# Cross attention on one core: a tile's first mixes held back, the finished tile's end spread over the next tile

## The chip, the cores and the metric

The kernel runs on one core of a Trainium2 chip: TensorE (matrix products), VectorE, ScalarE and GpSimd as compute engines, SyncE issuing the transfers. The metric is the device time of one launch in microseconds (us). Shown are the median of three runs and, for everything that is read in detail, one profiled execution.

## The reference, cut to what matters

A decoder of two layers on 4 x 256 tokens of width 256. The change touches one of its six blocks, the cross attention of layer 1. It treats all tokens as one sequence: 1024 queries against 1024 context rows, 16 heads of 16 columns.

```python
q = _fq_sym(q, axis=-1)          # rounded to 127 levels a head and token
k = _fq_sym(k, axis=-1)
v = _fq_sym(v, axis=2)
attn = jnp.einsum('bhqd,bhkd->bhqk', q, k)
attn = jax.nn.softmax(attn.astype(jnp.float32), axis=-1)
attn = _fq_unsigned(attn, axis=-1)   # rounded to 255 levels
out = jnp.einsum('bhqk,bhkd->bhqd', attn, v)
out = jnp.transpose(out, (0, 2, 1, 3)).reshape(B, N, C)
return out @ Wp + bp
```

The result is added to the residual stream x, whose normalised form feeds the routed experts.

## The kernel before, in words

`decoder` runs its blocks one behind the other. `cross_attention` (L1115) has two parts: `quantise` (L1133) makes the rounded queries, keys and values, and `attend` (L1309) does the rest. All of the change is in `attend`.

The 1024 queries are 8 tiles (NT) of 128. A unit u is one head of one tile: u = 16 t + h, 128 units in all. A unit passes through five stations:

- score (L1362, TensorE): two products of 512 columns, from the queries and keys of the head, into one of SCORED = 3 buffers of the accumulator memory. It waits until the exponential of unit u - 3 is done.
- row maximum and bias (L1424, VectorE): `c_neg_max` (L1427), then `c_bias` (L1429).
- exponential (L1416, ScalarE): scaled to 255 levels and written as 16-bit integers (`c_probs`), which rounds it; the sum of the row is read out behind it.
- cast (L1357, GpSimd) to bf16, then a transposing transfer (L1349, issued by SyncE) into `c_pT`, a ring of TURNED = 10 heads.
- mix (L1372, TensorE): eight small products (L1378) of the transposed head with the values, into 16 columns of `mixed`. The 16 heads of a tile fill 256 columns of one buffer, and there is only one such buffer.

When the 16 mixes of a tile are done, the tile is finished in five steps:

- `normalise` (L1432, VectorE): reciprocal of the row sums (L1434), and a multiply (L1438) that reads `mixed` and writes `c_o`. The first mix of the next tile waits for it (L1376), since it overwrites `mixed`.
- `finish_a` (L1382, TensorE): two turnings (L1387) into the buffer `tail`.
- `scale_values` (L1443, VectorE): two operations (L1448) from `tail` to `c_oT`.
- `finish_b` (L1390, TensorE): the projection in 32-bit floats (L1393) and its bias (L1394), into `tail` again.
- `residual` (L1451, VectorE): adds `tail` to x (L1453), then the statistics for the next normalisation (L94, L96).

Each engine works through its own list, which is written out by hand; the engines meet at semaphores alone. TensorE's list (L1396 to L1407) has for each u: score(u), then mix(u - 8) (MIX_LAG = 8), then, behind the mix of head 3 of a tile, `finish_a` of the tile before, and behind that of head 7 `finish_b`. VectorE's list (L1457 to L1469) has row_max(u), then behind unit 16 t + 8 `normalise`, behind 16 t + 11 `scale_values`, behind 16 t + 14 `residual`, each for tile t - 1. ScalarE, GpSimd and SyncE have nothing but the 128 units.

Of the kernel before, what the change touches and what calls it, by code (L numbers as in the profile page):

```python
# [18 lines left out]
NT = N // P  # L19
# [70 lines left out]
def norm_statistics(nc, eng, sh, t):  # L90


    ln = sh.ln
    nc.vector.bn_stats(ln.stats[:, t, :], sh.x[:, t, :]).then_inc(ln.steps, 1)  # L94
    if t >= 1:
        nc.vector.bn_aggr(ln.mv[:, t - 1, :], ln.stats[:, t - 1, :]).then_inc(ln.steps, 1)  # L96
        ln.step_count += 1
    ln.step_count += 1
    eng.wait_ge(ln.steps, ln.step_count)
    if t == NT - 1:  # L100
        nc.vector.bn_aggr(ln.mv[:, t, :], ln.stats[:, t, :]).then_inc(ln.steps, 1)
        ln.step_count += 1
        eng.wait_ge(ln.steps, ln.step_count)
        nc.vector.tensor_scalar(ln.rstd[:, :], ln.mv[:, :, 1], LN_EPS, None, ALU.add).then_inc(ln.var_ready, 1)  # L104
# [986 lines left out]
HEADS_C = 16  # L1091
# [23 lines left out]
def cross_attention(nc, sh, i):  # L1115
    with ExitStack() as ctx:
        sb, ps, sem = scope(nc, ctx, "c0_")
        s = Buffers()

        s.qT = sb("qT", [P, WC, N], BF16)  # L1120
        s.kT = sb("kT", [P, WC, N], BF16)
        s.v = sb("v", [P, NT, D], BF16)
        s.q_scale = sb("q_scale", [P, NT, HEADS_C])
        s.v_scale = sb("v_scale", [P, DC])
        s.identb = sb("identb", [P, P], BF16)
        s.w_p = sb("w_p", [P, DC, D])
        s.b_p = sb("b_p", [1, D])
        s.ones = sb("ones", [1, P])
        quantise(nc, sh, s, i)
        attend(nc, sh, s)  # L1130
# [178 lines left out]
def attend(nc, sh, s):  # L1309
# [4 lines left out]
    with ExitStack() as ctx:  # L1314
# [1 line left out]
        SCORED = 3  # L1316
        RING = 4
        ROUNDED = 6
        TURNED = 10
        MIX_LAG = 8  # L1320
        LOG_LEVELS = float(np.log(LEVELS_P))
        UNITS_C = NT * HEADS_C
        probs = sb("probs", [P, RING, N], I16)
        rounded = sb("rounded", [P, ROUNDED, N], BF16)
        pT = sb("pT", [P, TURNED, NT, P], BF16)
        neg_max, bias = sb("neg_max", [P, NT, HEADS_C]), sb("bias", [P, NT, HEADS_C])
# [5 lines left out]
        scored, bias_ready, exp_done, rounded_ready = sem("scored"), sem("bias_ready"), sem("exp_done"), sem("rounded_ready")  # L1332
        turned = [sem("turned%d" % n) for n in range(TURNED)]
        mixed_ready, o_ready, oT_ready, oT_copied, out_ready, out_added = (
            sem("mixed_ready"), sem("o_ready"), sem("oT_ready"), sem("oT_copied"), sem("out_ready"), sem("out_added"))

        def turned_count(u):

            return 16 * (u // TURNED + 1)

        block = ctx.enter_context(nc.Block())

        @block.sync
        def _(sp):
            for u in range(UNITS_C):
                sp.wait_ge(rounded_ready, u + 1)
                if u >= TURNED:
                    sp.wait_ge(mixed_ready, u - TURNED + 1)
                sp.dma_start_transpose(pT[:, u % TURNED, :, :], rounded[:, u % ROUNDED, :]).then_inc(turned[u % TURNED], 16)  # L1349

# [9 lines left out]
        @block.tensor  # L1360
        def _(pe):
            def score(u):  # L1362
                t, h = divmod(u, HEADS_C)
                if u >= SCORED:
                    pe.wait_ge(exp_done, u - SCORED + 1)
                at = slice(h % 2 * P // 2, (h % 2 + 1) * P // 2)
                for n in range(2):
                    last = nc.tensor.matmul(scores[:, u % SCORED, n, :], s.qT[at, h // 2, t * P:(t + 1) * P],  # L1368
                                            s.kT[at, h // 2, n * HALF:(n + 1) * HALF], start=True, stop=True)
                last.then_inc(scored, 1)  # L1370

            def mix(u):  # L1372
                t, h = divmod(u, HEADS_C)
                pe.wait_ge(turned[u % TURNED], turned_count(u))
                if h == 0 and t >= 1:
                    pe.wait_ge(o_ready, t)  # L1376
                for n in range(NT):
                    last = nc.tensor.matmul(mixed[:, 0, h * HD_C:(h + 1) * HD_C], pT[:, u % TURNED, n, :],  # L1378
                                            s.v[:, n, h * HD_C:(h + 1) * HD_C], start=(n == 0), stop=(n == NT - 1))
                last.then_inc(mixed_ready, 1)  # L1380

            def finish_a(t):  # L1382
                pe.wait_ge(o_ready, t + 1)
                if t >= 1:
                    pe.wait_ge(out_added, t)
                for c in range(DC):
                    last = nc.tensor.transpose(tail[:, 0, c * P:(c + 1) * P], o[:, c * P:(c + 1) * P], ident[:, :])  # L1387
                last.then_inc(oT_ready, 1)

            def finish_b(t):  # L1390
                pe.wait_ge(oT_copied, t + 1)
                for c in range(DC):
                    nc.tensor.matmul(tail[:, 0, 0:D], oT[:, c, :], s.w_p[:, c, :], start=(c == 0), stop=False)  # L1393
                nc.tensor.matmul(tail[:, 0, 0:D], s.ones[:, :], s.b_p[:, :], start=False, stop=True).then_inc(out_ready, 1)  # L1394

            for u in range(UNITS_C + MIX_LAG):  # L1396
                if u < UNITS_C:
                    score(u)
                if u >= MIX_LAG:
                    mix(u - MIX_LAG)  # L1400
                    t, h = divmod(u - MIX_LAG, HEADS_C)
                    if h == 3 and t >= 1:
                        finish_a(t - 1)
                    if h == 7 and t >= 1:
                        finish_b(t - 1)
            finish_a(NT - 1)
            finish_b(NT - 1)  # L1407
# [12 lines left out]
        @block.vector  # L1420
        def _(dve):
            chain = sh.chain.on(dve)

            def row_max(u):  # L1424
                t, h = divmod(u, HEADS_C)
                dve.wait_ge(scored, u + 1)
                chain.step(nc.vector.tensor_reduce(neg_max[:, t, h:h + 1], scores[:, u % SCORED, :, :].rearrange("p a b -> p (a b)"),  # L1427
                                                   AX.X, ALU.max, negate=True))
                nc.vector.tensor_scalar(bias[:, t, h:h + 1], neg_max[:, t, h:h + 1], s.q_scale[:, t, h:h + 1], LOG_LEVELS,  # L1429
                                        ALU.mult, ALU.add).then_inc(bias_ready, 1)  # L1430

            def normalise(t):  # L1432
                dve.wait_ge(exp_done, HEADS_C * (t + 1))
                chain.step(nc.vector.reciprocal(row_sum[:, t, :], row_sum[:, t, :]))  # L1434
                dve.wait_ge(mixed_ready, HEADS_C * (t + 1))
                if t >= 1:
                    dve.wait_ge(oT_ready, t)
                nc.vector.tensor_tensor(o[:, :].rearrange("p (h d) -> p h d", d=HD_C),  # L1438
                                        mixed[:, 0, 0:D].rearrange("p (h d) -> p h d", d=HD_C),
                                        row_sum[:, t, :].rearrange("p (h o) -> p h o", o=1).broadcast_to([P, HEADS_C, HD_C]),  # L1440
                                        ALU.mult).then_inc(o_ready, 1)

            def scale_values(t):  # L1443
                dve.wait_ge(oT_ready, t + 1)
                if t >= 1:
                    dve.wait_ge(out_ready, t)
                for c in range(DC):
                    last = nc.vector.tensor_scalar(oT[:, c, :], tail[:, 0, c * P:(c + 1) * P], s.v_scale[:, c:c + 1], None, ALU.mult)  # L1448
                last.then_inc(oT_copied, 1)

            def residual(t):  # L1451
                dve.wait_ge(out_ready, t + 1)
                nc.vector.tensor_tensor(x[:, t, :], x[:, t, :], tail[:, 0, 0:D], ALU.add).then_inc(out_added, 1)  # L1453
                dve.wait_ge(out_added, t + 1)
                norm_statistics(nc, dve, sh, t)

            for u in range(UNITS_C):  # L1457
                row_max(u)
                t, h = divmod(u, HEADS_C)
                if t >= 1:  # L1460
                    if h == MIX_LAG:
                        normalise(t - 1)
                    if h == MIX_LAG + 3:
                        scale_values(t - 1)
                    if h == MIX_LAG + 6:
                        residual(t - 1)
            normalise(NT - 1)
            scale_values(NT - 1)
            residual(NT - 1)  # L1469
# [459 lines left out]
```

## Time and profile before

| | |
|---|---|
| median of 3 runs | 1270.38 us (1269.29 to 1270.54) |
| the profiled execution | 1268.92 us |
| its span | 1267.1 us |
| `attend` in it | 862 to 1098 us, 236 us |
| the routed experts behind it | 1098 to 1267 us, 169 us |
| busy between 862 and 1098 us | TensorE 194.5 us, VectorE 189.1, ScalarE 165.8, GpSimd 133.2 |

The page gives busy time over the whole span, in which TensorE has 77% and VectorE 67%. For this change the stretch of `attend` counts: its table of stretches says how busy each engine was, at which TensorE clock (PEclk, 1.00 being full speed) and with which share of the transfer engines. In the timeline a row is one instruction or a few merged ones: start, duration, engine, line, operation and tiles, and in brackets how long the engine had stood idle and what released it. TensorE's rows appear twice, as PE (the product) and PEld (the load of its stationary operand). Matmul ends are modelled, so starts are what to go by.

### The profile page before, as it was taken

The page shows a single profiled execution, that of the slowest core. Times are in us where ns is not written, and L with a number is a line of the kernel's source. Part 1 is how long each engine was busy: PE and PEld are TensorE (multiplying, and loading weights), DVE is VectorE, ACT ScalarE, POOL GpSimd, SP SyncE. Part 2 cuts the span into 40 slices and gives each one's busy share as a digit, 9 for nine tenths or more (in the row PEclk, how much of TensorE's full clock was granted, in tenths as well). Part 3 has the DMA queues.
Part 4 walks back from the last instruction along what each step waited for, and adds up shares of the span by engine and source line. Part 5 has one row for each costly group of instructions (what it writes and reads, how often), then busy time and mean ns, then how long its engine had stood idle before and what let it go on. Part 6 is the DMA issues. An engine that isn't in the chain of part 4 may idle for free. (4 is left out here: it accounts for less than half of the span.)

```text
span 1267.1 us, 14674 instructions
## 1 busy us (share of the span) xinstructions
PE 978.5 (77%) x5537; PEld 647.1 (51%) x5537; DVE 852.1 (67%) x1192; ACT 598.8 (47%) x693; POOL 466.5 (37%) x278
## 2 busy tenths in 40 slices
PE   5669897349878889798989666877888888676990
PEld 2334743138777778687873255442222232355770
DVE  4663303999999999999702566687888788342442
ACT  2113032675866876777600233258777767311220
POOL 1133003855555555555000022205555555231004
PEclk9769989569898899898998979795555555568995
DMA  3020020000000000000002000946877876214113
GB/s 116 1 67 1 5 100 1 0 1 1 1 1 1 1 1 1 1 1 1 1 1 88 1 1 1 333 107 121 154 150 150 142 159 135 58 46 156 64 51 116
DMA packets 155448, 73.95 MB, mean 58 GB/s; under 512 B 138813, under 2 KB 151297, under 8 KB 154178
## 3 DMA queue, kind: packets, MB, share of 16 engines
q1 hardware_dynamic: 153842, 68.81, 21.5%
q0 software_dynamic: 1536, 4.20, 1.1%
q8 instruction: 45, 0.74, 0.2%
q14 instruction: 25, 0.20, 0.1%
HBM read 27.90 MB, written 11.53 MB: 31 GB/s over the span
## 5 line engine op out<-in xcount | busy, mean ns | idle before, releaser
L677 PE MATMUL r_head_sum<-ident,r_w 128*128 128x128 f32 (+1 forms) x2048 | 243.3, 283 | 41.7 <-DVE x L781 22.5
L677 PEld LDWEIGHTS r_head_sum<-ident,r_w 128*128 128x128 f32 (+1 forms) x2048 | 241.7, 199 | 48.4 <-issue 48.2
L631 POOL TENSOR_TENSOR r_pair_sum<-r_sims 128x2025 f32<-128x2025 f32 x39 | 142.1, 3646 | 148.8 <-DVE r_w L766 93.4
L1357 POOL CAST c_rounded<-c_probs 128x1024 bf16<-128x1024 int16 x128 | 133.2, 1040 | 156.2 <-ACT c_probs L1416 156.2
L1416 ACT ACTIVATE c_probs<-c_scores,c_bias,c_q_scale 128x1024 int16<-128x1024 f32 x128 | 154.2, 1205 | 61.3 <-DVE c_bias L1429 52.4
L1427 DVE TENSOR_REDUCE c_neg_max<-c_scores 128x1 f32<-128x1024 f32 x128 | 155.5, 1215 | 17.0 <-PE c_scores L1368 16.7
L775 DVE SCALAR_TENSOR_TENSOR r_w<-r_w,r_scale,r_z 128x2025 f32<-128x2025 f32 x64 | 148.0, 2314 | 7.9 <-PE r_z L645 7.0
L1368 PE MATMUL c_scores<-c_kT,c_qT 64*128 64x512 bf16 x256 | 129.9, 612 | 17.8 <-ACT c_probs L1416 14.3
L766 DVE SCALAR_TENSOR_TENSOR r_w<-r_pair_sum,r_kept,r_w 128x2025 f32<-128x2025 f32 x39 | 130.6, 3350 | 2.3 <-ACT r_w L703 2.2
L711 ACT ACTIVATE r_w<-r_w 128x2025 f32<-128x2025 f32 x64 | 116.1, 1882 | 4.2 <-DVE r_w L775 4.1
L1378 PEld LDWEIGHTS c_mixed<-c_v,c_pT 128*128 128x128 bf16 x1024 | 37.1, 106 | 124.8 <-issue 118.7
L703 ACT ACTIVATE r_w<-r_pair_sum,r_neg_max 128x2025 f32<-128x2025 f32 x39 | 76.8, 1981 | 34.4 <-PE r_head_sum L677 24.0
L653 PE MATMUL r_head_sum<-r_up,r_wT 128*128 128x256 f32 (+1 forms) x256 | 62.5, 406 | 16.1 <-ACT r_wT L731 16.1
L118 POOL TENSOR_TENSOR ln_rstd<-ln_rstd,ln_minus_half 128x8 f32<-128x8 f32 x6 | 9.9, 1646 | 163.8 <-DVE ln_rstd L104 155.5
L1378 PE MATMUL c_mixed<-c_v,c_pT 128*128 128x16 bf16 x1024 | 48.0, 177 | 23.4 <-DVE c_o L1438 17.4
L653 PEld LDWEIGHTS r_head_sum<-r_up,r_wT 128*128 128x128 f32 (+1 forms) x256 | 51.5, 204 | 25.5 <-ACT r_wT L731 17.8
L645 PE MATMUL r_z<-r_down,r_hT 128*128 128x512 f32 (+1 forms) x64 | 36.9, 729 | 32.5 <-DVE r_w L775 32.5
L631 POOL TENSOR_TENSOR xT<-r_sims 128x2025 f32<-128x2025 f32 x13 | 49.2, 3781 | 30.4 <-DVE r_w L766 30.4
L1791 DVE TENSOR_TENSOR e_gated<-e_hidden,e_gated 128x176 f32<-128x176 f32 x40 | 13.7, 342 | 65.7 <-ACT e_gated L1785 65.7
L631 POOL TENSOR_TENSOR ctxT<-r_sims 128x2025 f32<-128x2025 f32 x12 | 45.5, 3792 | 27.6 <-DVE r_w L766 27.6
L1686 POOL DMA_INDIRECT e_row<-expert_rows,e_place x16 | 15.3, 958 | 100.3 <-DMA expert_rows<-e_made 95.7
L1736 PE MATMUL e_hidden<-ew_w,e_rowT 128*128 x128 | 43.2, 460 | 0.0
(275 smaller groups left out, 1559.8 us busy)
## 6 DMA issues: line engine op xcount, KB each, us to landing
ew_w<-in_w SPq DMA_DIRECT2D x2, 2992.0 KB, 14.2
sorted_rows<-ew_w SPq DMA_DIRECT2D x1, 4096.0 KB, 40.2
e_row<-sorted_rows SPq DMA_DIRECT2D x8, 512.0 KB, 8.3
expert_rows<-e_made SPq DMA_DIRECT2D x8, 512.0 KB, 2.9
ew_w<-in_w_near SPq DMA_DIRECT2D x1, 2176.0 KB, 24.1
ctxT<-in_ctxT SPq DMA_DIRECT2D x2, 1024.0 KB, 8.8
r_up<-in_up SPq DMA_DIRECT2D x1, 2048.0 KB, 10.1
c_pT<-c_rounded SPq DMA_TRANSPOSE x128, 2.8
```

Source lines behind the costliest of these rows:

```text
L631: nc.gpsimd.tensor_tensor(sums[u % SUMS].rearrange("p (a b) -> p a b", b=KEYS), a.broadcast_to([P, KEYS, KEYS]), b.broadcast_to([P, KEYS, ...
L653: last = nc.tensor.matmul(head_sum[:, 0, 0:D], wT[0:k, b, :], r.up[0:k, b, :], start=(b == 0), stop=(b == PB - 1))
L677: last = nc.tensor.matmul(head_sum[0:m, b // 4, (b % 4) * P:(b % 4 + 1) * P], w[:, u % RING, b * P:b * P + m], ident[:, :], start=(h == 0 ...
L703: nc.scalar.activation(w[:, u % RING, :], sums[u % SUMS], ACT.Exp, bias=neg_max[:, t % 2, h:h + 1]).then_inc(exp_done, 1)
L711: nc.scalar.activation(w[:, u % RING, :], w[:, u % RING, :], ACT.Silu).then_inc(silu_done, 1)
L766: nc.vector.scalar_tensor_tensor(w[:, u % RING, :], sums[u % SUMS], kept[:, t % 2, h, TOP - 1:TOP], w[:, u % RING, :], ALU.is_ge, ALU.mult ...
L775: nc.vector.scalar_tensor_tensor(w[:, u % RING, :], w[:, u % RING, :], scale[:, t % 2, h:h + 1], z[:, :, :].rearrange("p a b -> p (a b)")[ ...
L1357: nc.gpsimd.tensor_copy(rounded[:, u % ROUNDED, :], probs[:, u % RING, :]).then_inc(rounded_ready, 1)
L1368: last = nc.tensor.matmul(scores[:, u % SCORED, n, :], s.qT[at, h // 2, t * P:(t + 1) * P], s.kT[at, h // 2, n * HALF:(n + 1) * HALF], sta ...
L1378: last = nc.tensor.matmul(mixed[:, 0, h * HD_C:(h + 1) * HD_C], pT[:, u % TURNED, n, :], s.v[:, n, h * HD_C:(h + 1) * HD_C], start=(n == 0 ...
L1416: nc.scalar.activation(probs[:, u % RING, :], scores[:, u % SCORED, :, :].rearrange("p a b -> p (a b)"), ACT.Exp, bias=bias[:, t, h:h + 1] ...
L1427: chain.step(nc.vector.tensor_reduce(neg_max[:, t, h:h + 1], scores[:, u % SCORED, :, :].rearrange("p a b -> p (a b)"), AX.X, ALU.max, neg ...
```

## The change

The first two mixes of a tile (HELD = 2) are left out at their place and done in pairs at heads 2 and 3: behind score 16 t + 10 come mixes 0 and 1, behind 16 t + 11 mixes 2 and 3, and from head 4 on it is one mix a unit again. `finish_a` goes from behind the mix of head 3 to behind that of head 4, `finish_b` from head 7 to head 9. On VectorE `normalise` stays behind row maximum 16 t + 8; `scale_values` goes from behind 16 t + 11 to 16 t + 14, and `residual` from 16 t + 14 to 16 t + 19, which is in the next tile; the one that falls off the end of the loop is done behind it. The ring of transposed heads grows from 10 to 13.

```diff
--- before.py
+++ after.py
@@ -1316,8 +1316,10 @@
         SCORED = 3
         RING = 4
         ROUNDED = 6
-        TURNED = 10
+        TURNED = 13
         MIX_LAG = 8
+        HELD = 2
+        TURN_AT, SCALE_AT, PROJECT_AT, ADD_AT = 4, 6, 9, 11
         LOG_LEVELS = float(np.log(LEVELS_P))
         UNITS_C = NT * HEADS_C
         probs = sb("probs", [P, RING, N], I16)
@@ -1334,6 +1336,14 @@
         mixed_ready, o_ready, oT_ready, oT_copied, out_ready, out_added = (
             sem("mixed_ready"), sem("o_ready"), sem("oT_ready"), sem("oT_copied"), sem("out_ready"), sem("out_added"))
 
+        def mixes_at(h):
+
+            if h < HELD:
+                return ()
+            if h < 2 * HELD:
+                return 2 * (h - HELD), 2 * (h - HELD) + 1
+            return (h,)
+
         def turned_count(u):
 
             return 16 * (u // TURNED + 1)
@@ -1397,11 +1407,12 @@
                 if u < UNITS_C:
                     score(u)
                 if u >= MIX_LAG:
-                    mix(u - MIX_LAG)
                     t, h = divmod(u - MIX_LAG, HEADS_C)
-                    if h == 3 and t >= 1:
+                    for m in mixes_at(h):
+                        mix(t * HEADS_C + m)
+                    if h == TURN_AT and t >= 1:
                         finish_a(t - 1)
-                    if h == 7 and t >= 1:
+                    if h == PROJECT_AT and t >= 1:
                         finish_b(t - 1)
             finish_a(NT - 1)
             finish_b(NT - 1)
@@ -1456,14 +1467,15 @@
 
             for u in range(UNITS_C):
                 row_max(u)
-                t, h = divmod(u, HEADS_C)
-                if t >= 1:
-                    if h == MIX_LAG:
+                if u >= MIX_LAG + HEADS_C:
+                    t, h = divmod(u - MIX_LAG, HEADS_C)
+                    if h == 0:
                         normalise(t - 1)
-                    if h == MIX_LAG + 3:
+                    if h == SCALE_AT:
                         scale_values(t - 1)
-                    if h == MIX_LAG + 6:
+                    if h == ADD_AT:
                         residual(t - 1)
+            residual(NT - 2)
             normalise(NT - 1)
             scale_values(NT - 1)
             residual(NT - 1)
```

## Rows read from the trace of the kernel before

**Rows 1.** Table of stretches: us; busy us (instructions) of each engine; PEclk; DMA share; GB/s.

```profile
880.00:890.00 10.00, 9.76 (x72) 2.99 (x72) 9.75 (x15) 9.41 (x15) 7.62 (x8) 0.50 0.95 170
944.00:972.00 28.00, 23.66 (x163) 8.24 (x161) 22.80 (x39) 19.76 (x32) 15.88 (x16) 0.50 0.73 150
```

**Rows 2.** Timeline, a unit at even pace: start us, us, engine, line, operation.

```profile
915.20 1.21 ACT L1416 ACTIVATE c_probs<-c_scores,c_bias,c_q_scale 128x1024 int16<-128x1024 f32 x1
...
916.46 1.21 DVE L1427 TENSOR_REDUCE c_neg_max<-c_scores 128x1 f32<-128x1024 f32 x1
...
916.55 1.03 PE L1368 MATMUL c_scores<-c_kT,c_qT 64*128 64x512 bf16 x2
...
917.71 0.21 DVE L1429 TENSOR_SCALAR c_bias<-c_neg_max,c_q_scale 128x1 f32<-128x1 f32 x1
917.84 1.21 DVE L1427 TENSOR_REDUCE c_neg_max<-c_scores 128x1 f32<-128x1024 f32 x1
```

**Rows 3.** Timeline, the normalising of a tile, and the next one's multiply.

```profile
924.74 0.24 DVE L1434 RECIPROCAL c_row_sum<-c_row_sum 128x16 f32<-128x16 f32 x1
...
925.02 0.42 DVE L1438 TENSOR_TENSOR c_o<-c_mixed,c_row_sum 128x256 f32<-128x256 f32 x1
...
925.59 0.36 PE L1378 MATMUL c_mixed<-c_v,c_pT 128*128 128x16 bf16 x8 [2.48 <-DVE c_o L1438]
...
926.95 1.22 DVE L1427 TENSOR_REDUCE c_neg_max<-c_scores 128x1 f32<-128x1024 f32 x1 [1.50 <-PE c_scores L1368]
...
928.46 1.21 ACT L1416 ACTIVATE c_probs<-c_scores,c_bias,c_q_scale 128x1024 int16<-128x1024 f32 x1 [2.30 <-DVE c_bias L1429]
...
953.98 0.42 DVE L1438 TENSOR_TENSOR c_o<-c_mixed,c_row_sum 128x256 f32<-128x256 f32 x1
```

**Rows 4.** Timeline, TensorE at its own pace, then turning and scaling.

```profile
927.16 1.03 PE L1368 MATMUL c_scores<-c_kT,c_qT 64*128 64x512 bf16 x2
...
928.44 1.03 PE L1368 MATMUL c_scores<-c_kT,c_qT 64*128 64x512 bf16 x2
...
930.24 1.03 PE L1368 MATMUL c_scores<-c_kT,c_qT 64*128 64x512 bf16 x2
...
931.09 0.60 DVE L1448 TENSOR_SCALAR c_oT<-c_tail,c_v_scale 128x128 f32<-128x128 f32 x2
```

**Rows 5.** Timeline, projection and residual of the first tile, and those of the seventh.

```profile
906.53 0.38 PE L1378 MATMUL c_mixed<-c_v,c_pT 128*128 128x16 bf16 x8
...
909.91 1.03 PE L1368 MATMUL c_scores<-c_kT,c_qT 64*128 64x512 bf16 x2
...
910.87 0.38 PE L1378 MATMUL c_mixed<-c_v,c_pT 128*128 128x16 bf16 x8
...
1080.70 1.20 ACT L1416 ACTIVATE c_probs<-c_scores,c_bias,c_q_scale 128x1024 int16<-128x1024 f32 x1
...
1083.73 0.42 DVE L1453 TENSOR_TENSOR x<-x,c_tail 128x256 f32<-128x256 f32 x1 [3.06 <-PE c_tail L1394]
...
1084.73 1.22 DVE L1427 TENSOR_REDUCE c_neg_max<-c_scores 128x1 f32<-128x1024 f32 x1
...
1086.23 1.21 ACT L1416 ACTIVATE c_probs<-c_scores,c_bias,c_q_scale 128x1024 int16<-128x1024 f32 x1 [4.24 <-DVE c_bias L1429]
```

**Rows 6.** List of waits, 860 to 1096 us: total us, times, longest us.

```profile
ACT c_probs L1416 <- DVE c_bias L1429: 52.4, 22, 4.2
DVE x L1453 <- PE c_tail L1394: 21.5, 7, 3.1
```

**Rows 7.** Table of stretches, the scores between a normalising and a turning.

```profile
928.00:934.00 6.00, 6.00 (x51) 2.14 (x50) 5.86 (x11) 4.78 (x7) 3.12 (x3) 0.50 0.69 152
```

**Rows 8.** Transposing transfers (ns min/median/max; landing), and the last mix in the timeline.

```profile
L1349 SPq DMA_TRANSPOSE c_pT<-c_rounded x128: 1231/1232/2688, 865.2 to 1088.7; - x128
...
DMA to landing us min/median/max: 2.7/2.8/5.3
...
1091.43 0.38 PE L1378 MATMUL c_mixed<-c_v,c_pT 128*128 128x16 bf16 x8 [5.13 <-DMA c_pT<-c_rounded]
```

## The prediction

> **What bounds the kernel now.** The table of stretches comes first. The attention stage runs from about 862 to 1098 us (the table of times), and the diff touches nothing outside it. While a tile's end is in the stretch (944 to 972 us), no engine is full: TensorE is busy 23.66 of 28 us, VectorE 22.80, ScalarE 19.76, the transfers 0.73 of the time. Between 880 and 890 us, where no finished tile is in the way, VectorE is busy 9.75 of 10 us [rows 1]. So the stage has an even pace and something that interrupts it.
>
> The timeline gives the pace [rows 2]. Row maxima start at 916.46 and 917.84, 1.38 us a head. VectorE sets it: row maximum, bias 1.25 us behind it (917.71), the next row maximum 0.13 us behind that, which is 0.08 us less than the bias's own 0.21 us. An exponential starts 1.50 us after its row maximum (926.95 to 928.46) [rows 3]. A score starts 1.35 us after the exponential three heads earlier (915.20 to 916.55), takes 1.03 us, and lies 1.29 us ahead of its row maximum (916.55 to 917.84). TensorE needs less than the pace when nothing holds it: 1.28 us from score to score (927.16 to 928.44) [rows 4], of which 0.96 goes by before the mix (909.91 to 910.87) [rows 5] and 0.32 is the mix.
>
> The timeline around a tile's end gives the interruptions, which have the same lengths in all seven tiles. First, normalising [rows 3]: VectorE is free at 924.74, and the next row maximum starts at 926.95, 2.21 us late; TensorE stood 2.48 us before the mix at 925.59, because the mix may not overwrite the sums that VectorE still reads, and the score is queued behind that mix. Second, scaling occupies VectorE from 931.09 for 0.60 us [rows 4], less the 0.08 us of hand-over: 0.52 us. Third, VectorE stands 3.06 us before the residual, waiting for the projection, which holds TensorE from the mix at 906.53 to the next score at 909.91; exponentials at 1080.70 and 1086.23 are 5.53 us apart, so 4.15 us are lost [rows 5]. Sum 6.88 us a tile; with 16 x 1.38 = 22.08 this is 28.96, and two normalisations are 925.02 and 953.98 apart, 28.96 [rows 3]. The list of waits agrees: ScalarE waited 52.4 us for the bias and VectorE 21.5 us for the projection [rows 6].
>
> **The change, part by part.** No instruction is added or removed; the arithmetic and the transfers are the same 128 heads. Only orders, and a ring of 13 instead of 10, change. I go through one tile with the figures above. Heads are counted on from the finished tile's successor: head 8 is the ninth of the new tile; head 16 on belong to the tile after.
>
> *Normalising, with the first two mixes held back.* VectorE's work keeps its place behind row maximum 8: 0.28 us from the reciprocal to the multiply (924.74 to 925.02) [rows 3], and then the multiply's 0.42 us less about 0.08 us of hand-over, 0.35 us; together 0.63 us, with 0.80 as the upper bound (full durations and a hand-over). The wait for it stood before score 9. It now stands behind score 10. Put score 8 at 0: row maximum 8 at 1.29, normalised tile ready at 1.29 + 1.38 + 0.28 + 0.42 = 3.37. Scores 9 and 10 start at 1.38 and 2.76, so the first mix asks at 2.76 + 0.96 = 3.72. It doesn't wait, but by only 0.3 us. Cost left: 0.63 instead of 2.21. The two held mixes are paid back as pairs, 0.96 + 2 x 0.32 = 1.60 us for heads 10 and 11; TensorE was ahead by 0.63 us because VectorE stood, so this hides. It costs if that lead is gone: 2 x 0.22 us.
>
> *Turning,* from behind mix 3 to behind mix 4. It put score 930.24 at 1.80 us behind score 928.44 instead of 1.28, so it costs 0.52 us of TensorE [rows 4]. Right after the pairs there is less lead than before: scores 10 to 13 start at 2.76, 4.36, 6.15, 7.95, and row maximum 13 can't start before 8.99, where VectorE was free at 8.82: 0.17 us lost.
>
> *Scaling,* behind row maximum 14: 0.52 us of VectorE, as before.
>
> *Projection,* from behind mix 7 to behind mix 9, that is behind score 17. Its length on TensorE is 909.91 - 906.53 - 0.32 = 3.06 us [rows 5]. Its stall is no longer behind VectorE's wait for the residual. Score 17 at 0: row maxima 17 and 18 are due at 1.29 and 2.67, but score 18 starts only at 0.96 + 0.32 + 3.06 = 4.34 and ends at 5.38: 2.71 us. From it goes the delay of 0.52 us that scaling has just put on VectorE, and which TensorE, 3 heads ahead at most, takes as lead: 2.19 us.
>
> *Residual,* now behind row maximum 19. It has its input, so VectorE spends its own work on it: 1083.73 to the next row maximum at 1084.73, 1.00 us [rows 5]. Before, this was hidden in the projection's stall; now it is paid, since after the stall TensorE makes a head per 1.28 us and VectorE is the late one again.
>
> *Sum for a tile:* 0.63 + 0.17 + 0.52 + 2.19 + 1.00 = 4.51, against 6.88; 22.08 + 4.51 = 26.6 us against 28.96. Both engines' own sums are under it: TensorE 16 x 1.28 + 0.52 + 3.06 = 24.1, VectorE 22.08 + 0.63 + 0.52 + 1.00 = 24.2. For the tile finished during the last one, projection and residual fall behind the last score; TensorE stands there anyway, 5.13 us before the last mix, for its transposed head [rows 8]. It pays 0.63 + 0.17 + 0.52 = 1.32. Saved: 6 x 2.37 + (6.88 - 1.32) = 14.2 + 5.6 = 19.8 us. The last tile's own end, from the exponential at 1086.23 on, is unchanged.
>
> *The ring of 13* lets held heads lie longer. A transpose waits for the mix 13 heads back instead of 10, and a mix is held back by two heads at most, so this wait is looser than now. Landing takes 2.8 us, 5.3 at most [rows 8]. A mix comes 1.35 + 5 x 1.38 + 0.96 = 9.2 us after its exponential starts; exponential, cast (less than a head's 1.38, since GpSimd keeps the pace) and landing take 1.35 + 1.38 + 2.8 = 5.5. Cost nothing, and nothing at 5.3 us either.
>
> *Bounds.* A paired mix can cost 0.32 to 0.40 us (0.38 is a mix's recorded length [rows 5]), which makes +3.3 us over the stage; the projection may overlap more or less, 2.7 to 3.4 us for 3.06, for -2 to +2; normalising at 0.80 makes +1.3. Together about -3 to +6 us on the sum.
>
> The profiled execution took 1268.92 us, 1.46 below the median of the runs. 1268.92 - 19.8 = 1249.1, and 1250.5 against the median.
>
> **Rivals.**
> *Clock.* All of this goes at TensorE's lower level, 1.2 GHz: granted clock 0.50 [rows 1]. If denser work raised it to 2.4 GHz, the projection would take about half (1.5 us) and its stall nearly vanish. The tile would cost 22.08 + 0.63 + 0.52 + 1.00 + about 0.2 = 24.4: saved 6 x 4.5 + 5.7 = 33 us, 1237. Against it: from 928 to 934 us TensorE was busy for 6.00 of 6.00 us, in this same mixture, and the clock stayed at 0.50 [rows 7].
> The Trainium skill, "TensorE: Matmul & The Clock Gate", Part 1 (The HAM clock gate), says that sustained TensorE activity lifts the throttle to 2.4 GHz; by that rule the result would be this rival's. The trace disagrees in that stretch, and I go with it.
>
> *The stall only moves.* If row maxima 18 and 19 come as late as row maximum 15 does now, for instance because the mixes and the projection leave TensorE no lead at all, the projection costs 4.15 and the residual 1.00 on top: 0.63 + 0.17 + 0.52 + 5.15 = 6.47 a tile, saved 6 x 0.42 + 5.6 = 8 us: 1262. Against: what made it 4.15 is that row maximum 15 waits behind a residual that waits for the projection, and this order is gone.
>
> *Transposes become the bound: slower.* They go through one queue, each waiting for its forerunner, and today's pauses let the queue drain: one landing took 5.3 us [rows 8]. With fewer pauses a backlog could reach the mixes. A landing must exceed 9.2 - 2.7 = 6.5 us to delay a mix, and the queue must need more than 26.6 / 16 = 1.66 us a head to set the pace, 28.96 / 16 = 1.81 to be slower than now; at 1.9 us the stage would take 7 x 1.4 = 10 us longer: 1280. Against: an issue takes 1.23 us (median; one took 2.69), the transfers' share between 880 and 890 us, at full pace, is 0.95, and the longest landing of the whole stage stayed under that.
>
> **How the numbers follow.** Forecast 0.82, clock 0.05, stall only moves 0.09, transposes 0.04. The forecast is the likeliest: 1250.5. Its bounds give 1247 to 1256; the range is 1245 to 1257, and the rivals lie outside with 0.18. A measurement of this kernel can tell about 0.2% (2.5 us) from no change. Faster: forecast, clock and the moved stall together 0.95; same 0.02 (a moved stall with the bounds against it), slower 0.03.
>
> **What would show it.** Normalisations 26.6 us apart. TensorE idle before a tile's first mix gone (2.48 us there, to nothing), VectorE's wait before the residual gone (21.5 us to almost nothing), and in its place row maxima that wait about 2.2 us for a score right after the projection. ScalarE's gaps about 0.6, 0.2, 0.5, 2.2 and 1.0 us a tile. The stage after keeps its 169 us. I am wrong if the mix waits for the normalised tile after all (its margin is 0.3 us), if the granted clock leaves 0.50, or if mixes wait for transposes.

## The result and the profile after

The changed kernel takes 1249.36 us (median of 4 runs, 1248.58 to 1250.83), against 1270.46 us before; the ratio is 0.9836, 95% interval 0.9819 to 0.9853. The forecast was 1250.5 us. The profiled execution took 1249.71 us, 19.2 us less than the profiled one of before, with a span of 1247.8 us.

| | before | after |
|---|---|---|
| `attend` in the trace | 862 to 1098 us, 236 us | 862 to 1078 us, 216 us |
| the routed experts behind it | 169 us | 170 us |
| two normalisations apart | 28.96 us | 26.64 us |
| ScalarE waited for the bias | 52.4 us | 33.9 us |
| VectorE waited at the residual, tiles 1 to 7 | 21.5 us | 1.9 us |
| TensorE waited for the normalised tile | 2.48 us a tile | 0 |

The whole difference lies in `attend`: from its first exponential to its last it takes 19.5 us less (223.4 us before, 203.9 after). The table of stretches of the kernel after, cut at its borders (the columns as in [rows 1]):

```profile
0.00:862.00 862.00, 666.68 (x3670) 492.86 (x3670) 600.28 (x688) 402.41 (x354) 299.37 (x111) 0.88 0.09 31
862.00:1078.00 216.00, 193.09 (x1338) 66.46 (x1338) 188.56 (x311) 165.74 (x256) 133.15 (x128) 0.50 0.79 157
1078.00:1247.80 169.80, 116.08 (x529) 86.27 (x529) 63.13 (x196) 30.44 (x83) 34.14 (x39) 0.80 0.25 81
```

Busy time is what it was, and the clock is still 0.50; only idle time went. Where it sat is seen by following one tile through the timeline of the kernel after, the counterpart of [rows 3]:

```profile
922.06 0.24 DVE L1445 RECIPROCAL c_row_sum<-c_row_sum 128x16 f32<-128x16 f32 x1
...
922.34 0.42 DVE L1449 TENSOR_TENSOR c_o<-c_mixed,c_row_sum 128x256 f32<-128x256 f32 x1
922.68 1.21 DVE L1438 TENSOR_REDUCE c_neg_max<-c_scores 128x1 f32<-128x1024 f32 x1
...
923.12 0.60 PE L1388 MATMUL c_mixed<-c_v,c_pT 128*128 128x16 bf16 x16
...
923.65 1.03 PE L1378 MATMUL c_scores<-c_kT,c_qT 64*128 64x512 bf16 x2
...
924.18 1.20 ACT L1427 ACTIVATE c_probs<-c_scores,c_bias,c_q_scale 128x1024 int16<-128x1024 f32 x1 [0.70 <-DVE c_bias L1440]
```

VectorE was free at 922.06, where the reciprocal starts. The next row maximum starts at 922.68, 0.62 us later, where it was 2.21 us [rows 3]. The pair of mixes (x16) starts at 923.12 with no wait in brackets. ScalarE's gap is 0.70 us instead of 2.30.

The projection and the residual of the same tile, further on in the timeline, against [rows 5]:

```profile
929.90 1.20 ACT L1427 ACTIVATE c_probs<-c_scores,c_bias,c_q_scale 128x1024 int16<-128x1024 f32 x1 [0.29 <-DVE c_bias L1440]
...
931.17 0.60 DVE L1459 TENSOR_SCALAR c_oT<-c_tail,c_v_scale 128x128 f32<-128x128 f32 x2
...
932.63 1.03 PE L1378 MATMUL c_scores<-c_kT,c_qT 64*128 64x512 bf16 x2
...
933.18 1.20 ACT L1427 ACTIVATE c_probs<-c_scores,c_bias,c_q_scale 128x1024 int16<-128x1024 f32 x1 [0.60 <-DVE c_bias L1440]
...
933.83 2.05 PE L1403 MATMUL c_tail<-c_w_p,c_oT 128*128 128x256 f32 x4
...
934.44 1.22 DVE L1438 TENSOR_REDUCE c_neg_max<-c_scores 128x1 f32<-128x1024 f32 x1
...
935.82 1.22 PE L1404 MATMUL c_tail<-c_b_p,c_ones 1*128 1x256 f32 x2
...
936.97 1.03 PE L1378 MATMUL c_scores<-c_kT,c_qT 64*128 64x512 bf16 x2
...
938.03 1.23 DVE L1438 TENSOR_REDUCE c_neg_max<-c_scores 128x1 f32<-128x1024 f32 x1 [2.13 <-PE c_scores L1378]
...
939.54 1.20 ACT L1427 ACTIVATE c_probs<-c_scores,c_bias,c_q_scale 128x1024 int16<-128x1024 f32 x1 [2.31 <-DVE c_bias L1440]
...
940.80 0.41 DVE L1464 TENSOR_TENSOR x<-x,c_tail 128x256 f32<-128x256 f32 x1
...
941.79 1.22 DVE L1438 TENSOR_REDUCE c_neg_max<-c_scores 128x1 f32<-128x1024 f32 x1
...
943.30 1.20 ACT L1427 ACTIVATE c_probs<-c_scores,c_bias,c_q_scale 128x1024 int16<-128x1024 f32 x1 [1.08 <-DVE c_bias L1440]
```

VectorE now stands at the row maximum of 938.03, 2.13 us, for a score, and not at the residual. The residual (940.80) waits for nothing and takes 0.99 us of VectorE's own time until 941.79; ScalarE pays it as a gap of 1.08. Each such gap contains the 0.08 us that ScalarE stands between two exponentials at even pace as well. The five gaps of a tile (0.70, 0.29, 0.60, 2.31 and 1.08 in the two cuts), less that, are 0.62, 0.21, 0.52, 2.23 and 1.00: 4.58 us, and 22.08 + 4.58 = 26.66, where two normalisations are 26.64 apart.

### The profile page after: what moved, and what is told of

Read it like the earlier page. It is cut to its first block and busy times, and to the rows that moved or that the text cites. A ratio compares the mean times of both kernels' runs of the same rounds, so it can differ in the third digit from the quotient of the medians.

```text
span 1247.8 us, 14671 instructions
## 1 busy us (share of the span) xinstructions
PE 975.9 (78%) x5537; PEld 645.6 (52%) x5537; DVE 852.0 (68%) x1192; ACT 598.6 (48%) x693; POOL 466.7 (37%) x278
## 5 line engine op out<-in xcount | busy, mean ns | idle before, releaser
L1427 ACT ACTIVATE c_probs<-c_scores,c_bias,c_q_scale 128x1024 int16<-128x1024 f32 x128 | 154.1, 1204 | 41.9 <-DVE c_bias L1440 33.9
L1378 PEld LDWEIGHTS c_scores<-c_kT,c_qT 64*128 64x128 bf16 x256 | 16.3, 106 | 52.7 <-ACT c_probs L1427 38.8
```

Source lines behind the costliest of these rows:

```text
L1427: nc.scalar.activation(probs[:, u % RING, :], scores[:, u % SCORED, :, :].rearrange("p a b -> p (a b)"), ACT.Exp, bias=bias[:, t, h:h + 1] ...
```

## The experiments

Each ran in four executions, next to seven of the kernel before (the change next to four). "A tile" is the distance of two normalisations in the middle of the stage. Rows are best compared by their ratios, since not all of them share the same seven.

| what runs | us | ratio to before, 95% interval | a tile, us |
|---|---|---|---|
| the change | 1249.36 | 0.9836 (0.9819 to 0.9853) | 26.64 |
| e1_held_only | 1260.44 | 0.9914 (0.9897 to 0.9930) | 27.38 |
| e2_spread_only | 1259.74 | 0.9917 (0.9900 to 0.9934) | 28.24 |
| e3_residual_in_stall | 1245.60 | 0.9801 (0.9784 to 0.9817) | 25.71 |
| e4_ring10 | 1251.02 | 0.9836 (0.9820 to 0.9853) | 26.64 |
| e5_half_projection | 1244.60 | 0.9791 (0.9775 to 0.9808) | 25.78 |
| e6_thirds | 1237.03 | 0.9731 (0.9714 to 0.9747) | 24.43 |
| e7_before_residual_later | 1258.67 | 0.9903 (0.9886 to 0.9921) | 27.62 |
| e8_lag6 | 1254.77 | 0.9875 (0.9858 to 0.9891) | 26.64 to 27.18, the first 28.37 |
| e9_full_rows | 1237.37 | 0.9740 (0.9724 to 0.9756) | 24.20 |
| e10_wide | 1240.35 | 0.9753 (0.9737 to 0.9769) | 24.21 |
| e11_thirds_wide | 1238.10 | 0.9739 (0.9723 to 0.9756) | 24.21 |

### Either half alone

The first leaves the five steps where they were and only holds the mixes back (the residual behind the end of VectorE's loop goes too, since it has its place inside again):

```diff
-        TURN_AT, SCALE_AT, PROJECT_AT, ADD_AT = 4, 6, 9, 11
+        TURN_AT, SCALE_AT, PROJECT_AT, ADD_AT = 3, 3, 7, 6
```

> Only the two mixes are held back (ring of 13); turning, scaling, projection and residual stay behind mix 3, row maximum 11, mix 7 and row maximum 14 as before. Theory of the sum: normalising costs 0.63 us instead of 2.21, scaling comes while TensorE has just made its pairs and turned, and projection with residual costs 4.15 again; stepped through head by head with the same figures, a tile takes 27.4 us and the program 1258.4. Rival, that a held mix gains nothing because the pairs cost TensorE what the wait did: 28.7 us a tile and about 1269. Rival, that holding back gives nearly all of the gain: 26.9 us and about 1252.

Measured: 27.38 us a tile, as the sum says, and 1260.44 us, 2.0 above the figure for the program. The gaps of ScalarE in a tile are 0.70, 0.60 and 4.24 us: the normalising has shrunk, the projection with the residual costs what it did.

The second leaves the mixes in place:

```diff
-        HELD = 2
+        HELD = 0
```

> No mix is held back (HELD = 0), the other places are those of the change. Theory of the sum: normalising costs 2.21 us again, and the steps behind it are as in the change: 28.2 us a tile, 1260. Together with the run that only holds back this says how much of the 21 us belongs to either part. If the parts were independent, the two gains would add up to 21 us; by the theory they give 12 and 10. Rival, that the later places gain nothing by themselves: 1269.

Measured: 1259.74 us, 28.24 us a tile; the gap of the normalising is 2.31 again. Each half is worth about 11 us against the kernel before, by the ratios 0.86% and 0.83%, and both together 1.64%: they add up within the intervals, and a tile says the same (1.58 and 0.72 us, together 2.32). That a tile says less of the second half (28.96 to 28.24) than the program does has the reason given in the prediction: in the last tile the projection and the residual fall behind the last score, which saves their 3.2 us once.

### Why the third loss was 4.15 us

The prediction put it down to the order on VectorE. One edit to the kernel before tests that:

```diff
-                    if h == MIX_LAG + 6:
+                    if h == MIX_LAG + 7:
                         residual(t - 1)
```

> The kernel before with one change: the residual one row maximum later (behind 16 t + 15, where it was behind 16 t + 14). Theory: the third loss of 4.15 us was made by the order, since row maximum 15 waited behind a residual that waited for the projection; one place later row maximum 15 is done during the projection and only the next one waits for its score: 27.6 us a tile instead of 28.96 and 1257. Rival, that TensorE's 3.06 us and the lost lead make the loss and VectorE's order doesn't matter: 1270.

Measured: 1258.67 us, 27.62 us a tile; the gap is 2.9 us. TensorE's work and its order are the same in both kernels. So of the 4.15 us about 1.3 were made by a row maximum that stood, with its score ready, behind a residual that waited. That bears out what the prediction held against the rival "the stall only moves"; the rival itself, with its 6.47 us of losses a tile and 1262 us, is refuted by the change's own 4.58 and 1249.36. A single moved line gives more than half of what the whole change gives, though not all of it by that 1.3 us: 6 x 1.34 = 8.0 us come from it, and 4.1 from the last tile (normalisations 22.05 us apart before, 17.91 here), where the waiting residual now stands behind the last row maximum and so the whole third loss is gone.

### The residual inside the stall

```diff
-        TURN_AT, SCALE_AT, PROJECT_AT, ADD_AT = 4, 6, 9, 11
+        TURN_AT, SCALE_AT, PROJECT_AT, ADD_AT = 4, 6, 9, 9
```

> As the change, but the residual stands behind row maximum 17 of a tile's count (ADD_AT = 9), not 19. Theory: the projection ends at about 4.5 us after score 17 starts, score 18 at 5.4, so VectorE does the residual (1.00 us) in the 2.2 us in which it waits for score 18 anyway, and of its 1.00 us some 0.1 is left: 25.7 us a tile and 1244.0, 5.4 us less than the change. Rival, the old order's trouble comes back (a residual that waits for the projection delays a row maximum that was ready): 27.6 us a tile or more, 1256.

Measured: 1245.60 us, 25.71 us a tile. The timeline of this kernel:

```profile
935.68 1.03 PE L1378 MATMUL c_scores<-c_kT,c_qT 64*128 64x512 bf16 x2
935.78 0.42 DVE L1464 TENSOR_TENSOR x<-x,c_tail 128x256 f32<-128x256 f32 x1 [1.17 <-PE c_tail L1404]
...
936.82 1.23 DVE L1438 TENSOR_REDUCE c_neg_max<-c_scores 128x1 f32<-128x1024 f32 x1
```

The score that follows the projection starts at 935.68 and would allow a row maximum at about 936.74 (1.06 us later, as from 936.97 to 938.03 in the kernel after); VectorE uses that time for the residual and is ready at 936.82. Of the 1.00 us some 0.1 is left: ScalarE's gaps of 2.31 and 1.08 us have become one of 2.38. The same wait for the projection that was harmful behind row maximum 14 in the kernel before is harmless here, because no finished score is queued behind it.

### Whose time the stall is

The projection without its second product:

```diff
-                for c in range(DC):
+                for c in range(1):
                     nc.tensor.matmul(tail[:, 0, 0:D], oT[:, c, :], s.w_p[:, c, :], start=(c == 0), stop=False)
```

> As the change, but the projection leaves out its second product (the second half of the columns; the output is not the reference's). Theory: the stall behind score 17 is TensorE's own time, so a tile gets shorter by the whole of that product, about 1.02 us (half of the 2.05 us that both take): 25.6 us a tile, 1242, and ScalarE's gap of 2.31 us goes to about 1.3. Rival, that the stall is a hand-over or a wait for the scaled tile: no more than 0.3 us a tile, 1248.

Measured: 1244.60 us, 25.78 us a tile, the gap 1.46 instead of 2.31. The stall is TensorE's own time; the rival's 0.3 us are refuted. But the product was sized wrongly, 0.86 us a tile and not 1.02. The timeline of this kernel shows why:

```profile
909.45 1.20 PE L1403 MATMUL c_tail<-c_w_p,c_oT 128*128 128x256 f32 x2
910.58 1.22 PE L1404 MATMUL c_tail<-c_b_p,c_ones 1*128 1x256 f32 x2
911.73 1.03 PE L1378 MATMUL c_scores<-c_kT,c_qT 64*128 64x512 bf16 x2
```

Ends are modelled, so the starts decide. One product goes by in 1.13 us (909.45 to 910.58) and two in 1.99 (933.83 to 935.82 above), so the second costs 0.86, what the tile lost; the recorded durations, 1.20 and 2.05 us, say 0.85. The first costs 0.27 us more than the second, for a reason that no run here shows, and half of the pair's duration counts a share of that into the product that was left out. From the first exponential to the last the trace has 5.1 us less than in the kernel after (198.8 and 203.9 us), six times 0.86; for the program 7.4 us less were expected and 4.8 measured.

### The projection in thirds

If VectorE's own work (24.2 us a tile) and TensorE's (24.1) are both under 26.6, the loss left is one of shape: a TensorE block of 3.06 us in one piece against a lead of a fraction of a head. So the three products go one by one to places where VectorE is late anyway:

```diff
-        TURN_AT, SCALE_AT, PROJECT_AT, ADD_AT = 4, 6, 9, 11
+        TURN_AT, SCALE_AT, ADD_AT = 6, 8, 19
+        PROJECT_AT, PROJECT_LAST = (11, 16, 19), (11, 12, 13)
...
-                    if h == PROJECT_AT and t >= 1:
-                        finish_b(t - 1)
+                    for c in range(DC + 1):
+                        at = PROJECT_LAST if t == NT - 1 and h >= MIX_LAG else PROJECT_AT
+                        done, off = divmod(u - MIX_LAG - at[c], HEADS_C)
+                        if off == 0 and done >= 1:
+                            finish_b(done - 1, c)
```

VectorE's loop is rewritten to match, with the scaling and the residual at their new places and one more of each behind the loop.

> As the change, but turning stands behind mix 6, scaling behind row maximum 16, and the projection's three parts are issued one by one: behind the mixes of head 11, 16 and 19 of the tile's count (11, 12 and 13 in the last tile), the residual behind row maximum 27 in units, that is head 19 of the count. Each part of about 1.02 us comes where VectorE is busy with normalising or scaling or the residual, so each hides in a delay that VectorE has anyway. Theory: nearly VectorE's own sum is left, 22.08 + 0.63 + 0.52 + 1.00 = 24.2, stepped through 24.4 us a tile: 1239. Rival, that a split projection loses more than it hides (each part with its own latency and a stall of 0.67 us at even pace): 26.1 us a tile and about 1247.

Measured: 1237.03 us, 24.43 us a tile. The computation is the same as before, and no other run has a lower median (e9 and e11 below lie within its interval): 12.3 us less than the change and 2.7% less than the kernel before. Its stretches, and below them those of the change:

```profile
900.00:1040.00 140.00, 138.61 (x973) 46.83 (x972) 135.30 (x223) 119.16 (x185) 95.48 (x93) 0.50 0.93 175
```

```profile
900.00:1040.00 140.00, 129.14 (x893) 44.13 (x892) 125.15 (x207) 109.35 (x171) 88.22 (x86) 0.50 0.80 160
```

TensorE goes from 129.14 to 138.61 busy us of 140, VectorE from 125.15 to 135.30. TensorE pays for the split, as the rival has it: each product alone goes by in 1.13 to 1.15 us, 3.4 for the three where the block takes 3.14 (933.83 to 936.97). But only about 0.2 us of it reach a tile: ScalarE's gaps, less 0.08, are 0.62, 1.00, 0.52 and 0.23. (The count of a tile's heads in the expectation is that of `mix`, 8 behind the score's.)

### The ring and the transposes

```diff
-        TURNED = 13
+        TURNED = 10
```

> As the change, but with a ring of 10 transposed heads instead of 13. Theory: the mix 10 heads back is done before a transpose is ready to go, also for the held ones (mix 0 comes behind score 10, its place is needed by the transpose of head 10, which is cast 4 us later), so the ring costs and gains nothing: 1249.4. Rival, that the longer ring is needed for the held mixes: the queue waits for a mix each tile, and every tile gets longer by up to 2 us: up to 1263.

Measured: 1251.02 us, next to a kernel before that took 1271.34: the ratio is that of the change to the fourth digit (0.9836), and so is the tile (26.64 us). The longer ring does nothing for the time.

```diff
-        MIX_LAG = 8
+        MIX_LAG = 6
```

> As the change, but a mix follows its score by 6 heads instead of 8, so it comes 6.4 us behind its exponential's start and not 9.2, and a landing of over 3.7 us delays it (at 8 heads over 6.5). Theory: transposes are far from a bound; the usual 2.8 us still pass, and only the few landings of 4 to 5 us show, each with less than 1.5 us: 1250 to 1255, with mixes waiting for transposes some 5 to 15 times. Rival, that the queue is near its limit at this pace: waits in each tile and 1260 or more.

Measured: 1254.77 us, at the upper end of what was expected. In the list of waits TensorE's weight loads wait 22 times and its products 8 times for a transpose, more often than forecast:

```profile
PEld c_mixed L1388 <- DMA c_pT<-c_rounded: 21.7, 22, 2.1
...
PE c_mixed L1388 <- DMA c_pT<-c_rounded: 6.1, 8, 2.0
```

Tiles are 26.64 us apart or, where mixes wait, up to 27.18; the first two normalisations are 28.37 apart, with a wait of 2.0 us of one mix between them. So the queue is no bound of the pace, but lateness is near: two heads less of distance already cost about 5 us. The slow rival of the prediction would have needed landings over 6.5 us; in the kernel after no transpose took longer than 4.7:

```profile
DMA to landing us min/median/max: 2.7/2.8/4.7
```

### The clock

In the run with thirds TensorE is busy 138.61 of 140 us, and the granted clock stays at 0.50, the level of 1.2 GHz. The scores use 64 of the array's 128 rows (64*128 in the rows). One edit uses all 128, on the kernel after:

```diff
-                at = slice(h % 2 * P // 2, (h % 2 + 1) * P // 2)
+                at = slice(0, P)
```

> As the change, but each score takes 128 rows of its operands instead of 64 (both heads of a pair are summed, so the output is not the reference's). Number, columns and order of the products are the same. Question: why does the granted clock stay at 0.50 although TensorE was busy 79.39 of 80 us in the run with the projection in thirds? Theory A, the clock doesn't rise because half of the array's rows lie idle in the scores: here it goes to 1.00 in this stage, the projection's stall almost vanishes, 24.4 us a tile and about 1235. Theory B, rows don't matter to it: granted clock 0.50 again, 26.6 us a tile and 1249.

Measured: 1237.37 us and 24.20 us a tile. The stretches of this kernel:

```profile
900.00:1040.00 140.00, 104.71 (x960) 53.58 (x961) 134.94 (x224) 118.80 (x185) 95.44 (x92) 0.73 0.90 175
```

The mean clock is 0.73: it changes between 0.50 (870 to 876 us) and 1.00 (957 to 959 us, at the projection below). It doesn't stay at 1.00, as Theory A had it. But it is up when it counts, as the timeline of this kernel shows at the projection:

```profile
957.26 0.35 PE L1388 MATMUL c_mixed<-c_v,c_pT 128*128 128x16 bf16 x8
957.47 1.11 PE L1403 MATMUL c_tail<-c_w_p,c_oT 128*128 128x256 f32 x4
958.51 0.69 PE L1404 MATMUL c_tail<-c_b_p,c_ones 1*128 1x256 f32 x2
959.13 0.61 PE L1378 MATMUL c_scores<-c_kT,c_qT 128*128 128x512 bf16 x2
```

From the mix to the next score it takes 1.87 us, against 3.38 before [rows 5], and ScalarE's gap there is gone from the second such tile on (the first two normalisations are 25.45 us apart, the others 24.20). With that Theory B is refuted.

Can it be had with the right scores? GpSimd writes each tile's queries out twice, times a mask that makes the other head's rows zero. The first tile keeps its 64 rows, the ring is the one of 10, which e4 showed to be worth nothing, and the filling of the mask and the waits are left out of this cut:

```diff
+                if h in (3, 9) and t < NT - 1:
+                    r = h // 9
+                    nc.gpsimd.tensor_scalar(wide[:, (t + 1) % 2, r, :, :], s.qT[:, :, (t + 1) * P:(t + 2) * P],
+                                            mask[:, r:r + 1], None, ALU.mult).then_inc(widened, 1)
...
-                    last = nc.tensor.matmul(scores[:, u % SCORED, n, :], s.qT[at, h // 2, t * P:(t + 1) * P],
+                    last = nc.tensor.matmul(scores[:, u % SCORED, n, :],
+                                            s.qT[at, h // 2, 0:P] if t == 0 else wide[:, t % 2, h % 2, h // 2, :],
```

> As the change (with the ring of 10), but from the second tile on each score takes 128 rows: GpSimd writes, twice a tile, the tile's queries times a mask, so that the rows of the other head of the pair are zero and the scores keep their values. Theory A, what raised the clock with 128 rows was that the rows are in use, zeros or not: granted clock about 0.7 and above in this stage, the projection nearly hidden, 24.3 us a tile, 1238. Theory B, zeros don't count: clock 0.50, 26.6 us a tile and 1250 plus what two more GpSimd operations a tile cost (they fit beside the casts, which leave 0.34 us a head, so at most 2 us in all).

Measured: 1240.35 us, mean clock 0.72, and 24.21 us for most tiles:

```profile
900.00:1040.00 140.00, 100.80 (x941) 53.07 (x958) 133.69 (x220) 117.47 (x181) 123.03 (x102) 0.72 0.98 172
```

Zeros do as well as data, and Theory A holds in that form: it isn't the changed values of e9 that raised the clock. What I missed is the price of the multiply:

```profile
L1376 POOL TENSOR_SCALAR c_wide<-c_qT,c_mask x14: 2837/2845/2856, 869.4 to 1024.8; 128x1024 bf16<-128x1024 bf16 x14
```

It takes 2.85 us, where the cast of as many elements takes 1.04. GpSimd is busy 123.03 of 140 us, and 0.98 is the share of the transfers. A cast behind a multiply comes late, and its transpose with it; besides, every transpose lands later, at least 3.1 and in the median 3.3 us after its issue (2.7 and 2.8 in the kernel after), for a reason that no run here shows. Mixes wait for one 27 times in TensorE's weight loads and 11 times in its products, against 2 and 2. Two distances of normalisations are longer than the others. In one (25.54 us) the clock was down at the projection (0.50 from 1006 to 1008 us). In the first (25.59) it was down for a part of the projection, and a mix waited for its transpose besides. The last tile is 18.42 us where e9 has 16.30, its last mixes waiting for transposes.

> The projection in thirds together with the 128-row scores of the run beside it. Theory: the tile is at VectorE's own sum already (24.4 us against 24.2), so a faster TensorE gives at most 0.2 us a tile: 1235 to 1237. Rival, that TensorE still holds back each head in some way that the thirds only hid: under 1232.

Measured: 1238.10 us, 24.21 us a tile. The edits are the two above together. By the program it doesn't differ from the thirds alone (1237.03): ratios 0.9739 and 0.9731 with overlapping intervals. A tile is 0.2 us shorter, as expected, and the two traces bear it out: from the first exponential to the last 189.0 us against 190.2. 1.1 us is too little to be seen in the medians of four executions. The rival (under 1232) is refuted: at 24.2 us VectorE's own work is the bound, whatever TensorE does.

## Why the prediction was right

*The five gaps.* Forecast 0.63, 0.17, 0.52, 2.19 and 1.00; measured 0.62, 0.21, 0.52, 2.23 and 1.00. The tile was forecast with 26.6 us, measured 26.64. The program was forecast with 1250.5, measured 1249.36; the profiled execution with 1249.1, measured 1249.71. Within the stage the saving was forecast with 19.8 us and is 19.5 in the traces: 14.0 (forecast 14.2) in the six distances of the first seven normalisations, and 5.54 (22.05 to 16.51; forecast 5.56) between the last two. The medians differ by 21.1 us; the interval of the ratio (18.7 to 23.0 us) holds both. What is above 19.5 isn't in the traced stage and is no merit of the sum.

*Normalising.* The mix doesn't wait, and its margin is what it was said to be: the tile was ready at 922.76 (922.34 + 0.42), the mix started at 923.12, 0.36 us later; the prediction's own terms give 3.72 - 3.37 = 0.35, which it rounds to 0.3.

*Paired mixes* were sized wrongly, without harm. A second mix was counted with 0.32 us and is about 0.21: the pair goes by from 923.12 to the score at 923.65 in 0.53 us, not 0.64. The bounds of 0.32 to 0.40 both lay above it, and the +3.3 us made from them don't follow: four paired mixes a tile with 0.08 us more in seven tiles are 2.2 us. It changed nothing because the score after the second pair waits for its exponential anyway.

*The projection's stall.* The step that took 0.52 off for the delay that scaling leaves is borne out. Score 17 starts 1.81 us ahead of its row maximum (932.63 and 934.44), where it is 1.29 at even pace: 0.52 us of lead. Without it the loss would be 2.71; e7, where the scaling lies further back, has 2.81, of which 0.08 are the residual that doesn't quite fit into the stall. e5 shows that the stall follows TensorE's time one for one.

*The residual.* The 1.00 us was right, but not what the prediction says of the kernel before, that this time "was hidden in the projection's stall; now it is paid". The rows of 1083.73 and 1084.73 [rows 5] show it paid there too: VectorE waited 3.06 us, had 0.08 of hand-over, and then spent 1.00 us on the residual before a row maximum whose score was ready, together 4.14 of the 4.15. The change leaves the 1.00 as it was and takes the waiting from 3.14 to 2.23. The sum doesn't suffer, since it sets the whole 4.15 against 2.19 + 1.00. It is e3 that hides the residual, down to 0.1 us.

*The last tile's extra* of about 3 us was in the sum; e2 shows it alone: its tiles are only 0.72 us shorter, six of them 4.3 us, and the last one was to save 6.88 - 2.21 - 0.17 - 0.52 = 4.0 us and saves 3.9 (22.05 to 18.12). That is 8.3 us, and in the trace it is 8.3 from the first exponential to the last. The profiled execution is shorter by 9.7 us of span; the other 1.4 lie outside that stretch, 2.2 less behind it and 0.8 more ahead of it.

*The clock rival* was rightly held against by the row of 928 to 934 us, and the stage kept 0.50. By the Trainium skill, "TensorE: Matmul & The Clock Gate", Part 1, sustained activity should have lifted it. The traces here don't agree: 140 us of nearly unbroken work with 64-row scores did not (e6, 138.61 us busy, 0.50), and 128-row scores, with less busy time, did in part (e9, 104.71 us busy, 0.73). The measurement decides. The price of that rival, 24.4 us a tile, was near (24.20).

*The bounds* were wider than they had to be: every term of a tile's sum came within 0.04 us of its value. They were also set loosely. The three upper ones add up to 6.6 us, where +6 is said, and the only lower one is -2, where -3 is said.

## What to carry to other kernels

When several engines pass units along with a lead of less than one unit, read each engine's even pace and its own work a period first; what is above the larger of the two is loss of shape. Here nearly all of it went away by cutting the block and putting each piece where another engine is late anyway (28.96 to 24.43 us, with the same instructions, against VectorE's own 24.2). Before a step that waits is put into an engine's list, look at what stands behind it: the same residual cost 1.3 us extra where a finished score was queued behind it, 1.0 us where it waited for nothing, and 0.1 us inside a stall that was there already. Stepping through one period with a handful of start-to-start distances from the timeline, checked first on the kernel at hand, gave each of the six orders for which a tile was forecast (the change, e1 to e3, e6, e7) within 0.1 us; where a product's own cost had to be guessed, in e5, it was off by 0.2.

## What the runs showed of the hardware that I had not expected

TensorE's granted clock stayed at 0.50 with the engine busy 138.61 of 140 us, as long as the scores used 64 rows of the array; with 128 rows, real or zero, the mean was 0.73 and 0.72, while the engine was busy only 104.71 and 100.80 us. A second 256-column product in 32-bit floats costs 0.85 us at the lower level, where one alone is recorded with 1.20. A second small mix behind a first costs 0.21 us and not the 0.32 from a mix to a score. On GpSimd, whose recorded durations are rough, a multiply of 128 x 1024 bf16 by a value a partition takes 2.85 us, a cast from int16 to bf16 of the same size 1.04.
